# Zone stage of a four-layer decoder: (sequence, zone) pairs sorted into tiles, and the order of loads in two sorted stages

## The reference

```python
xn = layernorm(x)                               # 64 sequences x 64 tokens x 128
logits = tanh(mean_over_tokens(xn) @ W1 + b1) @ W2 + b2     # 64 x 8, one row for each sequence
w = softmax over the 3 largest of the 8 logits, 0 for the other 5
x = x + xn + sum over zones z of w[:, z] * (gelu(xn @ Wa[z]) @ Wb[z])   # Wa: 128 x 512, Wb: 512 x 128
```

## Time and profile before

| | |
|---|---|
| median of three executions | 3717.55 us |
| profiled execution | 3717.75 us |
| its span, first to last instruction | 3716.0 us |
| mean granted TensorE clock (1.00 is 2.4 GHz, 0.50 is 1.2 GHz) | 0.898 |
| TensorE matmuls busy | 3009.2 us, 81% of the span |
| VectorE / ScalarE / GpSimd busy | 1999.4 / 1408.7 / 1362.3 us |
| DMA | 100.78 MB |

### The profile page before, as it was taken

One profiled execution on the slowest core, in us unless ns is written; L12 is line 12 of the kernel. 1 busy time (PEld: TensorE's weight loads), 2 busy tenths in 40 slices (PEclk: granted clock), 3 DMA queues, 4 the chain that ended last, 5 costly groups with the idle time before them and its releaser, 6 DMA issues. The chain is left out here.

```text
span 3716.0 us, 73067 instructions
## 1 busy us (share of the span) xinstructions
PE 3009.2 (81%) x29473; PEld 2054.4 (55%) x29473; DVE 1999.4 (54%) x4406; ACT 1408.7 (38%) x2320; POOL 1362.3 (37%) x1365
## 2 busy tenths in 40 slices
PE   4987779999899998988668878776677999982573
PEld 2554457777667775565423333244445988871573
DVE  2655442222267775663369899854565666653123
ACT  3432233333311111431166666643233666640333
POOL 2544420000032123535357677743453111115434
PEclk8988879999999998979889999998787999995897
DMA  7000000000000001003400000000000000001354
GB/s 255 2 1 1 1 1 1 1 1 1 6 2 3 3 3 40 13 4 99 121 0 1 1 1 1 0 1 1 1 2 10 5 8 8 2 2 57 123 175 130
DMA packets 66941, 100.78 MB, mean 27 GB/s; under 512 B 6896, under 2 KB 52336, under 8 KB 66032
## 3 DMA queue, kind: packets, MB, share of 16 engines
q1 hardware_dynamic: 59440, 81.34, 7.2%
q0 software_dynamic: 7168, 14.78, 1.1%
HBM read 79.23 MB, written 25.35 MB: 28 GB/s over the span
## 5 line engine op out<-in xcount | busy, mean ns | idle before, releaser
L661 POOL TENSOR_SCALAR arena<-arena 128x4 f32<-128x4 f32 x120 | 27.5, 229 | 1520.1 <-DVE arena L653 1269.6
L2439 POOL TENSOR_TENSOR arena<-arena 128x512 f32<-128x512 f32 x256 | 319.0, 1269 | 142.7 <-ACT arena L2370 142.0
L2500 DVE TENSOR_TENSOR_SCAN arena<-ps,arena 128x512 f32<-128x512 f32 x256 | 310.5, 1213 | 40.5 <-ACT ps L2381 23.4
L2252 PE MATMUL ps<-arena,const_w 128*128 128x512 f32 x512 | 278.2, 626 | 13.3 <-DVE arena L2508 12.3
L163 PEld LDWEIGHTS ps<-L_attn_w,arena 128*128 128x128 f32 x1984 | 242.4, 194 | 53.1 <-issue 42.3
L163 PE MATMUL ps<-L_attn_w,arena 128*128 128x128 f32 x1984 | 258.7, 281 | 8.0 <-POOL arena L2452 3.4
L163 PEld LDWEIGHTS ps<-L_ffn_w,arena 128*128 128x128 f32 x2176 | 251.6, 192 | 20.4 <-issue 19.9
L163 PE MATMUL ps<-L_ffn_w,arena 128*128 128x128 f32 x2176 | 256.5, 275 | 0.0
L788 ACT ACTIVATE arena<-ps 128x512 f32<-128x512 f32 x256 | 152.1, 597 | 274.1 <-PE ps L764 274.0
L798 DVE SCALAR_TENSOR_TENSOR x_all<-ps,arena,x_all 128x128 f32<-128x128 f32 x256 | 72.1, 344 | 326.9 <-PE ps L163 326.9
L764 PE MATMUL ps<-arena,L_ffn_w 128*128 128x512 f32 x512 | 233.2, 599 | 0.0
(11 more groups left out here) (415 smaller groups left out, 6611.2 us busy)
## 6 DMA issues: line engine op xcount, KB each, us to landing
arena<-pair_w SPq DMA_DIRECT2D x40, 578.0 KB
arena<-rt SPq DMA_DIRECT2D x24, 384.0 KB
pair_in<-pair_free SPq DMA_DIRECT2D x1, 5200.0 KB, 28.7
arena<-pair_in SPq DMA_DIRECT2D x40, 130.0 KB
L_ffn_w<-L_ffn SPq DMA_DIRECT2D x1, 4120.5 KB, 14.8
arena<-ctx SPq DMA_DIRECT2D x16, 256.0 KB, 3.1
arena<-pair_out SPq DMA_DIRECT2D x16, 256.0 KB, 5.1
L_attn_w<-L_attn SPq DMA_DIRECT2D x1, 3153.0 KB, 21.5
```

The lines of the kernel that those rows point to most:

```text
L2252: pe.matmul(acc(c), e.ident, hc(m, c), start=(k == 0), stop=(k == N - 1)).then_inc(s["acc_mm"], 1)
L2439: q.tensor_tensor(bu(m, c), du(g, c), bs(m), ALU.mult).then_inc(s["bu_done"], 1)
L2500: v.tensor_tensor_scan(hs(m, c), at(c), bu(m, c), 0.0, ALU.mult, ALU.add).then_inc(s["hs_done"], 1)
```

## The change

zone_ffn is rewritten. It norms all groups first, chooses three zones for each of the 64 sequences, and sorts the 192 pairs of sequence and zone by zone, each zone filled up to a multiple of four: at most 54 tiles of four sequences (256 tokens), of which always all 54 are run (a slot left over takes the first sequence with weight 0). VectorE computes the places (places()): for each of the 216 slots the sequence's first column (seqs), the weight (wtab), and for each tile the row of its zone's weights (rows). SyncE reads four entries of seqs per tile into registers and copies the four sequences from xnT_all to xT inside SBUF; it reads one entry of rows and loads 512 KB of weights from a new DRAM tensor zone_w; both have four buffers. TensorE makes four up and four down products of 256 columns per tile (down gives the result transposed), ScalarE two gelu steps of 512 columns, VectorE reads the same four entries into its registers and adds each sequence's result to acc at that column. In the end acc is transposed back and added to x. GpSimd clears acc and adds the normed x to x. L0_ffn's blob holds the tables in place of Wa and Wb.

In top1_ffn and top2_ffn SyncE's loop has load(t+4) ahead of the weights, and copy_ids runs two tiles ahead of its former place.

```diff
+ZK = 3
+ZU = 4
+NS = NG * NB
+ZT = (NS * ZK + E * (ZU - 1)) // ZU
...
+    T, U = ZT, ZT * ZU
+    TOK = ZU * S
...
+            def sequences(t):
+                if t < T:
+                    if t >= 4:
+                        sp.wait_ge(s["up_mm"], 2 * (t - 3))
+                    for u in range(ZU):
+                        first = sp.value_load(seqs[0:1, t * ZU + u:t * ZU + u + 1], min_val=0, max_val=(NS - 1) * S)
+                        sp.dma_start(xT(t)[:, u * S:(u + 1) * S], xnT_all[:, bass.ds(first, S)]
+                                     ).then_inc(fourth("x_in", t), 16)
+
+            def weights(t):
+                if t < T:
+                    if t >= 4:
+                        sp.wait_ge(s["down_mm"], t - 3)
+                    first = sp.value_load(rows[0:1, t:t + 1], min_val=0, max_val=(E - 1) * P)
+                    sp.dma_start(wt(t), e.zone_w[bass.ds(first, P), :]).then_inc(fourth("w_in", t), 16)
+
+            sp.wait_ge(s["rows_done"], 1)
+            weights(0)
+            sp.wait_ge(s["seq_done"], 1)
+            for t in range(4):
+                sequences(t)
+                if t:
+                    weights(t)
+            for t in range(T):
+                sequences(t + 4)
+                weights(t + 4)
...
+            def up(t):
+                if t < T:
+                    pe.wait_ge(fourth("x_in", t), 16 * ZU * (t // 4 + 1))
+                    pe.wait_ge(fourth("w_in", t), 16 * (t // 4 + 1))
+                    if t >= 2:
+                        pe.wait_ge(s["act_done"], 2 * (t - 1))
+                    for f in range(FC):
+                        ins = pe.matmul(e.bank(2 * (t % 2) + f // 2)[:, (f % 2) * TOK:(f % 2 + 1) * TOK],
+                                        wt(t)[:, f * P:(f + 1) * P], xT(t), start=True, stop=True)
+                        if f % 2:
+                            ins.then_inc(s["up_mm"], 1)
+
+            def down(t):
+                pe.wait_ge(s["act_done"], 2 * (t + 1))
+                if t >= 2:
+                    pe.wait_ge(s["acc_done"], ZU * (t - 1))
+                for f in range(FC):
+                    ins = pe.matmul(e.bank(4 + t % 2)[:, 0:TOK], wt(t)[:, (FC + f) * P:(FC + f + 1) * P],
+                                    hid(t)[:, f * TOK:(f + 1) * TOK], start=(f == 0), stop=(f == FC - 1))
+                ins.then_inc(s["down_mm"], 1)
...
+            p_.memset(acc, 0.0).then_inc(s["zeroed"], 1)
+            for g in range(NG):
+                ln.rstd(p_, g)
+                if g >= 1:
+                    p_.wait_ge(s["ln_xn"], NT * g)
+                    p_.tensor_tensor(e.X(g - 1), e.X(g - 1), xn(g - 1), ALU.add).then_inc(s["x_sum"], 1)
...
+                for z in range(E):
+                    places_z, w_z = pos[:, z:z + 1], lg[:, z:z + 1]
+                    part = tmp[0:NS, (z % 2) * 512:(z % 2) * 512 + U]
+                    if z == 0:
+                        own.step(v.tensor_scalar(q, W("slots")[0:NS, :], places_z, None, ALU.is_equal))
+                        own.step(v.tensor_scalar(qw, W("slots")[0:NS, :], places_z, w_z, ALU.is_equal, ALU.mult))
+                    else:
+                        v.scalar_tensor_tensor(out=q, in0=W("slots")[0:NS, :], scalar=places_z, in1=q,
+                                               op0=ALU.is_equal, op1=ALU.add)
+                        own.step(v.tensor_scalar(part, W("slots")[0:NS, :], places_z, w_z, ALU.is_equal, ALU.mult))
+                        own.step(v.tensor_tensor(qw, qw, part, ALU.add))
+                v.tensor_scalar(pos, pos, 0.0, None, ALU.mult).then_inc(s["q_done"], 1)
+                v.wait_ge(s["u_mm"], 1)
+                v.tensor_copy(seqs, seq_ps).then_inc(s["seq_done"], 1)
...
+            def summed(t):
+                first = [v.value_load(seqs[0:1, t * ZU + u:t * ZU + u + 1], min_val=0, max_val=(NS - 1) * S)
+                         for u in range(ZU)]
+                v.wait_ge(s["down_mm"], t + 1)
+                for u in range(ZU):
+                    k = t * ZU + u
+                    if k:
+                        v.wait_ge(s["acc_done"], k)
+                    place = acc[:, bass.ds(first[u], S)]
+                    v.scalar_tensor_tensor(out=place, in0=e.bank(4 + t % 2)[:, u * S:(u + 1) * S],
+                                           scalar=wtab[:, k:k + 1], in1=place, op0=ALU.mult, op1=ALU.add
+                                           ).then_inc(s["acc_done"], 1)
...
@@ -1026,9 +1143,9 @@
             for t in range(T):
-                weights(t + 3)
                 if t + 4 < T:
                     load(t + 4)
+                weights(t + 3)
@@ -1243,11 +1360,14 @@
+            copy_ids(0)
+            copy_ids(1)
             routed_gated(0)
             for t in range(T):
                 routed_gated(t + 1)
-                copy_ids(t)
                 copy_y(t)
+                if t + 2 < T:
+                    copy_ids(t + 2)
@@ -1316,9 +1436,9 @@
             for t in range(T):
-                weights(t + 4)
                 if t + 4 < T:
                     load(t + 4)
+                weights(t + 4)
```

More of the change, by code:

```diff
@@ new lines, in zone_ffn @@
+        fourth = lambda name, t: s[f"{name}{t % 4}"]
+        ln = PipedNorm(e, s, room, e.X, xn, 1e-5, dstT=xnT, bank=e.bank(7))
+        pooled, hr = room.take(NS), room.take(NS)[0:32, :]
+        small = room.take(15 * E)[0:NS, :]
+        lg, keep, count, pad, ends, offs, pos, here = (small[:, i * E:(i + 1) * E] for i in range(8))
+        mx, tot, steps = small[:, 64:65], small[:, 65:66], room.take(E * 16)
+        ends_all, pad_all, offs_all, cnt_all, ex = (room.take(n) for n in (E, E, E, E, T))
@@ new lines, in _ @@
+            pe.wait_ge(s["q_done"], 1)
+            pe.matmul(seq_ps, W("first"), q, start=True, stop=True)
+            pe.matmul(w_ps, e.ones[0:NS, :], qw, start=True, stop=True).then_inc(s["u_mm"], 1)
+            pe.wait_ge(s["w_done"], 1)
+            up(0)
+            for t in range(T):
+                up(t + 1)
+                down(t)
+            for g in range(NG):
+                if g == 0:
+                    pe.wait_ge(s["acc_done"], ZU * T)
+                transpose_group(pe, e, e.bank(g), acc[:, g * GT:(g + 1) * GT]).then_inc(s["z_mm"], 1)
@@ L867, in _ @@
[L867 to L872, removed]
+            for g in range(NG):
+                ln.copy(a, g)
+            a.wait_ge(s["r1_mm"], 1)
+            a.activation(hr, r1, ACT.Tanh, bias=W("b1"), scale=1.0 / S).then_inc(s["r1_act"], 1)
@@ L892, in weights @@
[L892 to L898, removed]
-            for step in (lambda g: ln.stats(v, g), lambda g: ln.scale(v, g), pool, logits, weights):
-                step(0)
@@ L902, in _ @@
[L902 to L918 removed]
+                v.tensor_reduce(pooled[:, g * NB:(g + 1) * NB], tiles(xnT(g), NB), AX.X, ALU.add
+                                ).then_inc(s["pool_done"], 1)
@@ new lines, in _ @@
+            own.step(v.memset(one8, 1.0))
+            for g in range(NG):
+                ln.stats(v, g)
+                if g >= 1:
+                    scale(g - 1)
+                if g >= 2:
+                    pool(g - 2)
+            scale(NG - 1)
+            pool(NG - 2)
+            pool(NG - 1)
+            choice()
+            places()
+            v.wait_ge(s["zeroed"], 1)
+            for t in range(T):
+                summed(t)
+            v.wait_ge(s["x_sum"], NG)
+            for g in range(NG):
+                v.wait_ge(s["z_mm"], g + 1)
+                v.tensor_tensor(e.X(g), e.bank(g), e.X(g), ALU.add)
```

156 lines of the change are left out of this document (81 added, 75 removed).

## The result

| | before | after |
|---|---|---|
| median of four executions each, side by side | 3717.48 us | 3566.22 us (3564.07 to 3569.85) |
| profiled execution / its span | 3717.75 / 3716.0 us | 3569.85 / 3567.4 us |
| mean granted TensorE clock | 0.898 | 0.879 |
| DMA moved | 100.78 MB | 132.19 MB |

The account below looks back on a forecast made before the run. The prediction took TensorE's matmuls to bound the old zone stage, and SyncE's issues the new one. From 3717.8 us it took 113 (zone stage), 9.5 (setup), 37 (top2_ffn) and 12 (top1_ffn): 3546 us, range 3480 to 3625.

Parts of the forecast that it names:

- SyncE as the bound: Zone loop: SyncE's five registers and DMAs set 5.6 us per tile (5.2 to 6.3), 54 tiles, 302 us.
- Ahead of the loop: Zone stage: norms, router and choice, counts and places take 48.5 us until SyncE may start.
- Behind it: Zone stage after the loop: last weights and tile 8.5 us, then turning back and adding eight groups 6.7 us.
- VectorE: Zone loop: four registers 2.4 us and four sums 2.0, together 4.4 us per tile, under SyncE's 5.6.
- Clock and DMA: Zone loop: DMA needs about 2.1 us per tile, hidden; only a granted clock below 0.62 would show.
- Setup: L0_ffn's blob loses 3.90 MB, so the wait for setup loads shrinks: -9.5 us.
- top2_ffn: Row loads ahead of weights remove the waits for pair_in: -37 us, bounds -45 and 0.
- top1_ffn: Row loads first, ring of three weight buffers still limiting: -12 us; waits for rt replace those for moe_in.
- 1: Zone loop: VectorE's registers cost 1.3 us each and set 7.2 us per tile: +86, 3632 us; chance 0.15.
- 2: Zone loop: VectorE's registers make the kernel slower than before, 9.7 us per tile, 3770 us; chance 0.05.
- 3: Zone loop: SyncE's five issues overlap; TensorE or DMA sets 3.9 us per tile: -92, 3454 us; chance 0.10.
- 4: top1_ffn and top2_ffn: row loads first do nothing, weights and rows landing together: +49, 3595 us; chance 0.10.

Follow-up runs that it names:

- e2: Changed kernel with the register and DMA of the zone stage's weights issued by ScalarE instead of SyncE: 3502.0 us.
- e3: Changed kernel with SyncE copying sequences from fixed columns, no registers for them, so not the chosen sequences: 3459.0 us.
- e5: Changed kernel with two of a zone tile's four sequences issued by SyncE and two by ScalarE: 3454.3 us.
- e4: Changed kernel with VectorE adding sums at fixed columns, no registers, so to other sequences than those chosen: 3561.1 us.
- e1: Changed kernel with the old order of loads and place of copy_ids back in top1_ffn and top2_ffn: 3616.6 us.
- e9: Changed kernel with e5's split issue and four buffers of weights in top1_ffn, three rounds: 3452.7 us, ratio to before 0.9288.
- e12: Changed kernel with four buffers of weights in top1_ffn instead of three, timed in three rounds: 3566.2 us, ratio to before 0.9596.
- e7: Changed kernel with row loads still first but copy_ids back in its former place: 3569.9 us.
- e10: e9 with VectorE's registers read without bounds, three rounds: 3470.3 us.
- e11: Changed kernel with SyncE's registers for the sequences read without bounds: 3584.4 us.
- e6: e5 and e4 together, split issue and sums at fixed columns without VectorE registers: 3431.4 us.

## Why the prediction was right, and where not

**SyncE as the bound: right; its pace 9% too small.** e2, e3 and e5 each speed the stage up by taking issue work from SyncE, and e4 shows that VectorE's registers count for nothing in the loop until then. The term that was mis-sized is the pair of register and DMA, taken as 1.12 us from the earlier trace rows. There the DMAs read DRAM. The DMA instruction alone adds 0.519 - 0.36 = 0.16 to it, and an instruction that only the DMA from DRAM has ahead of it (0.03, with its gap 0.07) falls away: 1.12 + 0.16 - 0.07 = 1.21. The prediction had seen the second and not the first. Its 0.52 for a DMA with no register was misread as well: the last of the four took 0.47 by itself, not 0.36, so they are (1.93 - 0.47) / 3 = 0.49 apart; the 0.6 us of a register comes out either way. Its bounds for the tile, 5.2 to 6.3, held the 6.1. The loop took 571.9 to 900.9, 329 us instead of 301: **28 of the 31 us** by which the stage, 396 in place of 365, missed.

**Ahead of the loop: right.** 48.5 us forecast; from 524.7 to SyncE's first register at 571.9 it is 47.2. GpSimd's clearing of acc took 3.51 (3.8 forecast from the earlier trace rows); the first up product came 53 us after the first bn_stats (55).

**Behind it: 5.4 us too little.** The turning back took 6.2 us (6.7 forecast), but from the last weights' issue at 900.9 to the first of these adds at 914.75 there are 14 us, not 8.5. The last tiles arrive closer together than VectorE's 4 us, so its sums (903.62, 907.93, 911.90) queue: once SyncE has nothing left to issue, the next slowest engine sets the pace. e4 bears it out: with no registers on VectorE this end of the stage is 4.4 us shorter.

**VectorE: right in the sum.** 4.0 us against the 4.4 taken; the register is 0.62 (0.6), the sum with its moving address 0.43 (0.51).

The Trainium skill, "DMA: Bandwidth & Descriptors", section "Latency and other measured facts", has about 600 ns as the floor of a tensor_load. The instruction takes 0.27 us on SyncE and 0.30 on VectorE here. A whole register, with the arithmetic and the assertion that follow the load, takes 0.6 us on both: the page's figure fits that sum, and the trace does not bear it out for the load alone.

**Clock and DMA: right.** The granted clock was 0.91 in the loop with TensorE busy 68% of it, and the DMA share 0.36. Neither sets the pace.

**Setup: right.** The first bn_stats comes at 40.91 us instead of 49.84, -8.9 against -9.5.

**top2_ffn: the mechanism right, the size 12 us too small.** The waits row was taken for the whole of the gain. But the loop went from 200 to 153 us, 47 less: TensorE's idle time fell by 38.9 - 1.0 = 37.9, and its busy time by 161.1 - 152.0 = 9.1, for the same products. The mean of an up product fell from 401 to 386 ns, and that of a turn from 300 to 281. So a wait costs more than its own length. Part of it is the end of the products ahead of the wait, which the next ones overlap when there is none: down(t) is busy 1.95 us, but the next turn starts 1.78 after it. Another part is the clock: 27 of the 320 records of an up product took some 634 ns instead of 379 before, in four groups, and 8 in one group after. Whether the waits brought the lower clock about is not shown. The bound of -45 was nearer than the value taken.

**top1_ffn: the sum right, its parts not.** -11.9 against -12. The loop gave 7.4 (92.9 to 85.5 us), and e1 gives it back (93.3). Another 3.5 came from the scatter (44.6 to 41.1), which the prediction did not have, and which is 45.1 to 47.0 in e9 to e12 with the same text: it varies between executions. So the -11.9 hit the forecast by luck. The tiles took 3.02 and 3.94 us in turn, 3.57 in the mean from the second on, just above the 3.2 to 3.55 worked out from the earlier trace rows. "Waits for rt" never appeared under that name; the shorter loops with four buffers show that the ring was the cause all the same.

**The rivals.** 1 and 2 (VectorE) fell by e4, though e3 and e5 show that VectorE is next, at 4.0 us. 3 fell: the issues add up (e2). 4 fell by e1.

**Misses among the expectations.** e7, e9, e10, e11 and e12. Two (e10, e11) rest on one mistake, that leaving out the bounds of a register removes instructions. e9 and e12 rest on another: 12 us of one execution (0.3%) were taken for an effect on the time, against the bound of 0.5% that the prediction itself had set.

## What to carry to other kernels

Where tiles are fed at places read from registers, count the issuing engine's time per tile first: here a register and a copy inside SBUF cost 1.22 us of SyncE, five issues outweighed TensorE's 3.46 us of products, and sharing them between two issuing engines was worth 112 us of 3566. Take the price of an issue from one of the same kind, not from one that reads DRAM. In a queue, what is needed first and has the longest way goes first: exchanging two lines in SyncE's loop gave 45 us in top2_ffn. A single execution can't prove 12 us.

## What the runs showed of the hardware

- A DMA instruction holds the issuing engine for 0.52 us if it copies 128 rows of 256 bytes inside SBUF with its address in a register; with fixed addresses and four in a row (e3) for 0.47 the first and 0.60 the others. From DRAM it is 0.37 for 128 rows of 4096 bytes and 0.375 for 256 rows of 516 bytes. The copies inside SBUF land 1.8 us after issue (the median on the page of after).
- Two engines can issue copies side by side with hardly a loss: in e5 and e6 two copies on SyncE mostly took 1.73 us, as 1.22 + 0.52 in after, while ScalarE issued two more. The DMA instruction took 0.52 us on SyncE and 0.53 on ScalarE (medians), and over 0.7 in 2 of 216 (e5).
- An engine's registers are hidden in its idle time in the profile: 2.5 us of them per tile on VectorE are shown as a wait for TensorE (e5), and are worth 0.5 us per tile only once they are the bound (e6).
